# First cross attention of a two-layer Perceiver block: the row of negated maxima is turned by VectorE and moved within SBUF instead of by TensorE, and the first value group of a head comes one pair later

## The reference, cut to what matters

```
def _L0_xattn_ref(qkv, y):
    N_HEADS = 16
    bs, width, length = qkv.shape                 # 1, 256, 512
    ch = width // N_HEADS                         # 16
    q = qkv.reshape(bs * N_HEADS, ch, length)
    k = v = y.reshape(bs * N_HEADS, ch, -1)       # 16 heads, 16 channels, 8192 positions
    scale = 1.0 / math.sqrt(math.sqrt(ch))
    weight = jnp.einsum('bct,bcs->bts', q * scale, k * scale)
    weight = jax.nn.softmax(weight.astype(jnp.float32), axis=-1).astype(weight.dtype)
    a = jnp.einsum('bts,bcs->bct', weight, v)
    return a.reshape(bs, -1, length)

x = x + _L0_xattn_ref(_layernorm(x, axis=-1), ctx_2048)
```

## Time and profile before

| | us |
|---|---|
| median of three runs | 1475.16 |
| the profiled execution, its own time | 1478.31 |
| its span (first to last instruction) | 1476.5 |
| first cross attention within it | 0 to about 711 |
| TensorE matmul busy | 1403.7 (95%) |
| VectorE busy | 1164.5 (79%) |
| ScalarE busy | 947.5 (64%) |
| GpSimd busy | 108.3 (7%) |

### The profile page before, as it was taken

How to read it: one execution, slowest core, us unless ns; L and a number is a source line. 1 busy time by engine, 2 the same in 40 slices (tenths; PEclk the granted TensorE clock), 3 DMA queues, 4 the chain that set the end, 5 groups by cost and what they waited for, 6 DMA issues and landing times. The chain is left out here.

```text
span 1476.5 us, 27007 instructions
## 1 busy us (share of the span) xinstructions
PE 1403.7 (95%) x10741; PEld 856.7 (58%) x10741; DVE 1164.5 (79%) x1623; ACT 947.5 (64%) x1754; POOL 108.3 (7%) x99
## 2 busy tenths in 40 slices
PE   3999999999999999999898999999989889998998
PEld 1533333333333333334357899999967764567998
DVE  6999999999999999984576666666667457886665
ACT  0288888888888888889184455455423632775453
POOL 8301111111111011100000000000000000000000
PEclk9999999999999999999999999999999999999999
DMA  7434465554444433445204655545354522103640
GB/s 172 110 48 101 106 161 142 142 136 103 103 112 86 110 83 102 102 73 72 86 1 174 241 176 195 184 175 195 143 234 179 228 121 107 65 1 129 220 184 25
DMA packets 34910, 189.20 MB, mean 128 GB/s; under 512 B 7624, under 2 KB 8048, under 8 KB 22768
## 3 DMA queue, kind: packets, MB, share of 16 engines
q1 hardware_dynamic: 34608, 187.49, 42.3%
q10 hardware_dynamic: 192, 0.20, 0.1%
HBM read 163.23 MB, written 21.27 MB: 125 GB/s over the span
## 5 line engine op out<-in xcount | busy, mean ns | idle before, releaser
L448 DVE TENSOR_REDUCE pm<-bank 128x1 f32<-128x1024 f32 x512 | 618.2, 1223 | 16.5 <-PE bank L540 13.7
L510 ACT ACTIVATE probs<-bank 128x512 f32<-128x512 f32 x1024 | 551.2, 598 | 64.5 <-PE bank L557 6.1
L540 PE MATMUL bank<-kst,qst 50*128 50x512 f32 x1024 | 368.3, 459 | 27.3 <-DMA qst<-qsplit 20.3
L557 PE MATMUL bank<-qst,kst 50*128 50x512 f32 x1024 | 364.2, 446 | 1.6 <-DVE pm L448 0.8
L570 PE MATMUL bank<-probs,vext 128*32 128x256 f32 x3840 | 306.5, 391 | 1.9
L557 PEld LDWEIGHTS bank<-qst,kst 50*128 50x128 f32 x1024 | 150.5, 184 | 207.7 <-ACT probs L510 189.1
L1219 PE MATMUL bank<-e_xhi,e_hi 128*128 128x256 f32 (+1 forms) x784 | 221.4, 282 | 0.3 <-DVE e_xlo L1283 0.3
L1219 PE MATMUL bank<-e_xhi,e_lo 128*128 128x256 f32 (+1 forms) x784 | 221.5, 283 | 0.0
L1219 PE MATMUL bank<-e_xlo,e_hi 128*128 128x256 f32 (+1 forms) x784 | 221.5, 282 | 0.0
L570 PEld LDWEIGHTS bank<-probs,vext 128*32 128x32 f32 x3840 | 76.0, 107 | 174.3 <-issue 97.9
L540 PEld LDWEIGHTS bank<-kst,qst 50*128 50x128 f32 x1024 | 148.3, 189 | 42.8 <-DVE pm L448 20.6
(11 more groups left out here) (220 smaller groups left out, 1538.6 us busy)
## 6 DMA issues: line engine op xcount, KB each, us to landing
raw<-wall SPq DMA_DIRECT2D x34, 1536.0 KB, 6.5
kst<-kscratch SPq DMA_DIRECT2D x192, 128.0 KB, 4.3
raw<-wall SPq DMA_DIRECT2D x10, 2304.0 KB, 8.7
kscratch<-ksplit SPq DMA_DIRECT2D x15, 1024.0 KB, 4.0
kraw<-ctx_rows SPq DMA_DIRECT2D x16, 512.0 KB, 4.1
vraw<-ctx_vt SPq DMA_DIRECT2D x16, 512.0 KB, 5.0
ctxT<-ctxT SPq DMA_DIRECT2D x8, 1024.0 KB, 11.6
nat<-ctx_chunks SPq DMA_DIRECT2D x6, 1024.0 KB, 21.8
```

The source lines that it names most:

```text
L448: nc.vector.tensor_reduce(pm[:, h % 2, r % 4, r // 4:r // 4 + 1], bank[:, 2 * (r % 2):2 * (r % 2) + 2, :], AX.XY, ALU.max).then_inc(pre_re ...
L510: nc.scalar.activation(probs[:, (XT * h + n) % PR, :], bank[:, bank_of(h, n), :], ACT.Exp, scale=XSCALE).then_inc(probs_ready, 1)
L540: ins = nc.tensor.matmul(bank[:, 2 * (r % 2) + j, :], qst[64 * j:64 * j + KR, h, tt * P:tt * P + P], kst[64 * j:64 * j + KR, h % 2, c * 51 ...
L557: nc.tensor.matmul(bank[:, bank_of(h, n), :], kst[64 * j:64 * j + KR, h % 2, m * P:m * P + P], qst[64 * j:64 * j + KR, h, :], start=True, ...
```

## The change

`turn` goes from TensorE. VectorE turns `nsplit` (now 128 x 32, its first eight columns filled) as 32x32 blocks and copies the four blocks next to each other into `nturned`, on partitions 0 to 31; SP moves the eight rows with two DMAs into `qst` (`stack_negmax`). The two copies from PSUM go, and with them the place of its own in the rotation of banks. VectorE's block of five stands ahead of its reduction r = 1. The first half of the first value group of a head moves from the end of step 10 to between the two pairs of step 11.

```diff
@@ setup
-    identr = at(172.5, "identr", [P, P], F32R)
-    nsplit = at(173, "nsplit", [P, 4, NSW], F32R)
+    nsplit = at(172.5, "nsplit", [P, 2, 32], F32R)
+    nblocks = at(172.75, "nblocks", [P, 32])
+    nturned = at(173, "nturned", [32, 2, P], F32R)
@@ SP
+            def stack_negmax(h):
+
+                sp.wait_ge(negmax_turned, h + 1)
+                for j in range(2):
+                    sp.dma_start(qst[64 * j + 32:64 * j + 34, h, :].bitcast(F32), nturned[0:8, h % 2, :].bitcast(F32)).then_inc(negmax_stacked, 16)
@@
                     load_q(h + 1)
+                    if h > 0:
+                        stack_negmax(h)
                     load_stack(h + 1, 1)
@@ VectorE
-            def stack_negmax(h):
-
-                dve.wait_ge(negmax_turned, h + 1)
-                nc.vector.tensor_copy(qst[96:98, h, :], bank[96:98, s_bank(h - 1, TURN_AT), :]).then_inc(negmax_stacked, 1)
+            def turn_negmax(h):
+
+                dve.wait_ge(nsplit_step, 2 * h + 2)
+                if h >= 2:
+                    dve.wait_ge(negmax_stacked, 32 * (h - 1))
+                link(nc.vector.transpose(nblocks[:, :], nsplit[:, h % 2, :].bitcast(F32)))
+                for q in range(4):
+                    ins = nc.vector.tensor_copy(nturned[:, h % 2, 32 * q:32 * q + 32], nblocks[32 * q:32 * q + 32, :])
+                ins.then_inc(negmax_turned, 1)
@@
-                    if h >= 1 and r == TURN_UNIT:
-                        stack_negmax(h - 1)
+                    if h >= 1 and r == 1:
+                        turn_negmax(h - 1)
@@ ScalarE
-                    if n == TURN_AT and h < XH - 1:
-                        stack_negmax(h + 1)
@@ TensorE, score
-                elif slot == TURN_AT + 3:
-                    pe.wait_ge(negmax_stacked, 2 * h + 4)
-                elif h > 0 or slot >= 3:
-                    pe.wait_ge(probs_ready, XT * h + (slot if slot < TURN_AT + 3 else slot - 1) - 2)
+                elif h > 0 or n >= 3:
+                    pe.wait_ge(probs_ready, XT * h + n - 2)
@@ TensorE, the window of a head
                 for i in range(XP):
-                    if i == TURN_UNIT:
-                        turn(h)
                     for e in range(2):
                         late_score(h, 2 * i + e)
                         pre(h + 1, i, 1 - e)
+                        if e == 0 and i == FIRST_V + 1:
+                            late_values(h, FIRST_V)
...
-                    late_values(h, i)
+                    if i != FIRST_V:
+                        late_values(h, i)
```

More of the change, by code:

```diff
@@ L34 @@
 XG = XT // 4
-XSLOTS = XT + 1
 PR = 12
@@ L38 @@
 Q_ROWS = [(0, 0), (XC, 0), (2 * XC + 2, 1)]
-NSW = 98
 LAGP = 7
 PVLAG = 2
-TURN_UNIT = 4
-TURN_AT = 2 * (XP + TURN_UNIT - LAGP)
+FIRST_V = LAGP + 1 + PVLAG
 S_BANKS = [4, 5, 7]
@@ L249, in cross_attention_0, with s_bank @@
     x_final = sem("x_final")
[L251 to L256, removed]
+    def s_bank(h, n):
+        return S_BANKS[(XT * h + n) % 3]
     def bank_of(h, n):
-        return LAST_BANKS[n % len(LAST_BANKS)] if h == XH - 1 else s_bank(h, place(n))
+        return LAST_BANKS[n % len(LAST_BANKS)] if h == XH - 1 else s_bank(h, n)
     def chunk(n):
@@ L332, in _ @@
                     load_v(1)
+                    stack_negmax(0)
                 if h == XH - 1:
@@ L401, in _ @@
             pool.wait_ge(const_set, 10)
-            nc.gpsimd.tensor_copy(identr[:, :], ident[:, :]).then_inc(g.ident_ready, 1)
+            nc.gpsimd.tensor_copy(g.identb[:, :], ident[:, :]).then_inc(g.ident_ready, 1)
             pool.wait_ge(g.ident_ready, 3)
-            nc.gpsimd.tensor_copy(g.identb[:, :], ident[:, :]).then_inc(g.ident_ready, 1)
-            pool.wait_ge(g.ident_ready, 4)
             nc.gpsimd.memset(nsplit[:, :, :].bitcast(F32), 0.0).then_inc(const_set, 1)
@@ L412, in _ @@
                 pool.wait_ge(negmax_ready, h + 1)
[L413 to L416, removed]
+                if h >= 2:
+                    pool.wait_ge(negmax_turned, h - 1)
+                nc.gpsimd.tensor_copy(nsplit[:, h % 2, 0:4], negmax[:, h % 2, :]).then_inc(nsplit_step, 1)
                 pool.wait_ge(nsplit_step, 2 * h + 1)
-                nc.gpsimd.tensor_tensor(nsplit[:, :, 33:98:64], both, nsplit[:, :, 32:97:64].bitcast(F32),
+                nc.gpsimd.tensor_tensor(nsplit[:, h % 2, 4:8], negmax[:, h % 2, :], nsplit[:, h % 2, 0:4].bitcast(F32),
                                         ALU.subtract).then_inc(nsplit_step, 1)
@@ L451, in _ @@
                 nc.vector.tensor_reduce(negmax[:, h % 2, :], pm[:, h % 2], AX.X, ALU.max, negate=True).then_inc(negmax_ready, 1)
-            stack_negmax(XH - 1)
+            turn_negmax(XH - 1)
             dve.wait_ge(split_stored, 16 * XH)
@@ L484, in copy_o @@
                 nc.scalar.copy(osb[:, h % 2, :], bank[:, 6, :]).then_inc(o_copied, 1)
-            def stack_negmax(h):
-                act.wait_ge(negmax_turned, h + 1)
-                nc.scalar.copy(qst[32:34, h, :], bank[32:34, s_bank(h - 1, TURN_AT), :]).then_inc(negmax_stacked, 1)
             act.wait_ge(g.ident_ready, 2)
@@ L501, in _ @@
                                         qsplit[0:XC, part, 0, :].bitcast(F32)).then_inc(stack_lo[0], 16)
-            stack_negmax(0)
             for h in range(XH):
                 for n in range(XT):
-                    if n == TURN_AT and h < XH - 1:
-                        stack_negmax(h + 1)
                     act.wait_ge(scores, XT * h + n + 1)
@@ L517, in _ @@
         def _(pe):
[L518 to L526, removed]
             def pre(h, r, j):
@@ L545, in score @@
             def score(h, n):
-                m, j, slot = n // 2, n % 2, place(n)
+                m, j = n // 2, n % 2
                 if n == 0:
-                    pe.wait_ge(negmax_stacked, 2 * h + 2)
+                    pe.wait_ge(negmax_stacked, 32 * (h + 1))
                 if h == XH - 1:
@@ L611, in first_busy @@
                     for j in range(2):
-                        nc.tensor.matmul(bank[:, 4 + j, :], qst[64 * j:64 * j + KR, h, 0:P], kst[64 * j:64 * j + KR, h, 0:512],
+                        nc.tensor.matmul(bank[:, 4 + j, :], kst[64 * j:64 * j + KR, h, 0:P], kst[64 * j:64 * j + KR, h, 0:512],
                                          start=True, stop=True)
@@ L620, in _ @@
             pe.wait_ge(const_set, 12)
-            pe.wait_ge(g.ident_ready, 3)
             for h in range(XH - 1):
                 for i in range(XP):
-                    if i == TURN_UNIT:
-                        turn(h)
                     for e in range(2):
@@ L638, in _ @@
             for i in range(LAGP):
-                if i == TURN_UNIT:
-                    turn(last)
                 for e in range(2):
```

## The result

The changed kernel takes 1483.12 us (median of 5 runs, 1481.27 to 1484.01) against 1475.16 (median of 5, 1474.77 to 1477.12): ratio 1.0053, 95% interval 1.0042 to 1.0064. It is slower, by 8.0 us, as forecast (1483).

A forecast was written before the change was run, and what follows sets the result against it. TensorE's order was taken as the bound. 14 x (-0.49 turn + 0.55 block + 0.51 moved group) = +8.0, window 0 +0.3, last window -0.5: +7.8 us on the median of 1475.16, so 1483 us; range 1473 to 1489.

The forecast's parts named there:

- The bound: Whole head: TensorE's own order sets the pace, at 1.23 us a step; VectorE and ScalarE have slack.
- The turn: TensorE, each of 16 windows: taking the turn off it saves 0.49 us.
- The block: VectorE ahead of reduction r = 1: transpose and four copies take 0.90 us, less 0.35 slack; TensorE stands 0.55 at step 3.
- The moved group: TensorE, steps 10 and 11: score n = 8 waits 0.61 us for activation n = 5; costs 0.51 us a head.
- The low end of the moved group: Steps 10 and 11, rival: score behind the value group isn't held, -0.19 us a head instead of +0.51; chance 0.10.
- Window 0: First window: block costs 0.14 us and the order 0.11, with no gain from the turn; +0.3 us.
- the order: TensorE, steps 10 and 11: the new sequence alone, with the score not held, costs 0.11 us more.
- The DMAs: Moving the turned rows: landed at about 305.7, first score at 306.9; hidden, with 1.2 us to spare.
- The sum: Whole run: windows 1 to 14 +8.0 us, first window +0.3, last window -0.5; total +7.8 us.

The follow-up runs named there:

- act_half: The kernel before, with activations over 256 instead of 512 columns (but for the first twelve); 1474.22 us.
- values_back: The changed kernel, with the first half of a head's first value group back at the end of step 10; 1475.92 us, ratio 1.0009.
- pool_copies: The changed kernel, with the four 32x32 copies on GpSimd and only the transpose left on VectorE; 1474.31 us, ratio 0.9995.
- same_quadrant: The changed kernel, with all four copies reading the block on partitions 0 to 31; 1477.62 us.
- before_moved: The kernel before, with only the first half of the first value group moved between the pairs of step 11; 1483.49 us, ratio 1.0059.
- copy5: The changed kernel, with ScalarE's copy of the old result behind activation n = 5 instead of n = 4; 1477.28 us, ratio 1.0023.
- late_block: The changed kernel, with VectorE's block of five ahead of its reduction r = 4 instead of r = 1; 1481.12 us.
- pool_back: The changed kernel, with the four copies on GpSimd and the first value group back at the end of step 10; 1468.26 us, ratio 0.9952.

## Why the prediction was right

- **The bound.** TensorE's own order at 1.23 us a step: `act_half` shows it, and the variants that took a gap out of TensorE gave back about that gap a head: 0.51 for 0.49 (`values_back`), 0.42 for 0.52 (`pool_copies`) and 0.22 for 0.31 (`same_quadrant`), the last two with the longer of the two steps told of below.
- **The turn, -0.49.** `pool_copies` has no stall left at step 3; from a head's last maximum to its reduction r = 10 it takes 12.31 us, against 12.78 before: -0.47.
- **The block, 0.90 long, stall 0.55.** Measured 0.88 and 0.52, and both go with the four copies. The transpose (0.20 alone, 0.24 to the first copy) was priced from a reciprocal with a wait behind it. The held copies were at 0.20 each and measure 0.18.
- **The moved group, +0.51.** Measured +0.49 in the changed kernel. Without the new block it is as much at its place (`before_moved`, 0.93 from pair to pair), and the head grows by 0.58, 0.06 of it by the longer step.
- **The low end of the moved group, -0.19, was too low.** It left out that the `pre` beside the score waits for VectorE too; in `copy5` it takes 2.84 us from reduction r = 10 to r = 12, against 2.77 before, 0.07 more and not 0.19 less. The range had taken in a case that this run doesn't bear out.
- **Window 0, +0.3, was mis-sized.** It measures +0.85: 0.66 goes with the group (`values_back`), where I had put 0.11. VectorE sets the pace of that window up to step 11, at 1.13 a reduction, and the `pre` of step 11 waits for it, in the changed kernel at 71.56:

```profile
71.56 0.49 PE L528 MATMUL bank<-kst,qst 50*128 50x512 f32 x1 [0.35 <-DVE pm L454]
71.97 0.64 PE L556 MATMUL bank<-probs,vext 128*32 128x256 f32 x8
72.55 0.50 PE L543 MATMUL bank<-qst,kst 50*128 50x512 f32 x1
```

At its old place the value half lies in this wait. Behind it both halves are TensorE's alone, so that steps 10 and 11 take 3.13 us (70.42 to 73.55) against 2.46 in `values_back` (70.52 to 72.98). I had priced the order there and not the wait: it is the same loss as in the other windows, with VectorE in ScalarE's place.

- **The DMAs, hidden.** I had the rows 1.2 us early with 4.1 to landing; `late_block` measures 2.5 for the way from the last copy to use, issues included, where I had 0.9 + 4.1 = 5.0. So in the changed kernel they are ready at 304.71 + 2.5 = 307.2, and the first score is at 305.90 + 4 x 1.23 = 310.8: 3.6 to spare.
- **The sum, +7.8**, came to +8.0. In the profile it is 14 x 0.52 + 0.85 - 0.49 = +7.6, and 0.5 of a later first maximum. Between the executions profiled, that maximum moved between 57.9 and 59.1 whatever the variant, so this isn't the change's. Window 0 short by 0.55 and the windows over by 14 x 0.05 cancelled, and that the sum meets the time to 0.2 us is luck in this part.

## What to carry to other kernels

Where engines hand over in lockstep, work inserted in one of them costs its length less the lead that its consumer leaves it (0.35 us here), so work out this lead before moving work off the bound engine; many small instructions spend it quickly. Moving an instruction away from a wait only helps if what takes its place isn't behind the same wait: here the value group filled the time in which the next score was held anyway. And check a releaser in a list of waits: look up when the very instruction waited for had ended, and make the named engine faster.

## What the runs showed of the hardware that I had not expected

- Four 32x32 casts on VectorE start 0.18 us apart when they read from successive groups of 32 partitions and 0.09 apart when they all read the first.
- Four such casts on GpSimd take 0.98 us together, and moving eight rows by two DMAs takes 2.5 us from the last copy to the first matmul that uses them, 1.36 of it SP's issue of the two.
- The steady step has two values, 1.230 and 1.233 us, constant within a head: from the third window on, before, the changed kernel, `values_back` and `late_block` have the first, `before_moved`, `pool_copies` and `same_quadrant` the second, `pool_back` and `act_half` both in turn by head, `copy5` both without such an order. It is 0.06 us a head, some 0.9 us a run, and accounts for most of what heads of 40.75 and 40.27 have above the expected 40.66 and 40.17. Its cause stays open.
